# Slot bounds for four last sequences, chunk lists one by one, and another order of the first expert's start

## The reference

```python
x = layernorm(x + attention(x, w_q, w_k, w_v, w_o))   # 16 heads of 16 features
gates = softmax(x_flat @ gating_w)                    # 8 experts
topk_w, topk_idx = top_k(gates, 2)
position = cumsum(onehot(flat_e)) - 1                 # place of an entry in its expert's list
valid = position < capacity                           # capacity 1280
h = relu(einsum('ecd,edh->ech', buf, w1) + b1)        # hidden 1024
out_e = einsum('ech,ehd->ecd', h, w2) + b2
out_flat[flat_t] += out_e[flat_e, position] * w_eff   # 0 where not valid
x = layernorm(x + out_flat)
```

## Time and profile before

| | us |
|---|---|
| median of 3 runs (lowest, highest) | 818.85 (818.65, 819.21) |
| the profiled execution's own time | 818.66 |
| its span, first to last instruction | 816.8 |
| PE busy | 770.8 (94% of the span) |
| VectorE (DVE) busy | 605.0 (74%) |
| ScalarE (ACT) busy | 443.3 (54%) |
| GpSimd (POOL) busy | 406.4 (50%) |

### The profile page before, as it was taken

One profiled execution on the slowest core, in us unless ns is written; L12 is line 12 of the kernel. 1 busy time (PEld: TensorE's weight loads), 2 busy tenths in 40 slices (PEclk: granted clock), 3 DMA queues, 4 the chain that ended last, 5 costly groups with the idle time before them and its releaser, 6 DMA issues.

```text
span 816.8 us, 16628 instructions
## 1 busy us (share of the span) xinstructions
PE 770.8 (94%) x5919; PEld 642.9 (79%) x5919; DVE 605.0 (74%) x1325; ACT 443.3 (54%) x753; POOL 406.4 (50%) x595
## 2 busy tenths in 40 slices
PE   7689999999999988889999999999999999999993
PEld 6567777777777755778898898888988988988993
DVE  6757888888888898968657568568568567575982
ACT  3166777777777777645345345335435344444670
POOL 2000166665665547664364464462552553546774
PEclk9789999999999999999999999999999999999998
DMA  6567766565555672443352442452542532434841
GB/s 162 117 165 168 172 160 142 130 150 119 121 121 114 125 194 58 156 149 79 83 109 41 97 110 42 95 110 40 108 100 38 143 53 78 104 52 66 317 167 48
DMA packets 71535, 93.89 MB, mean 115 GB/s; under 512 B 11949, under 2 KB 55886, under 8 KB 71325
## 3 DMA queue, kind: packets, MB, share of 16 engines
q1 hardware_dynamic: 53308, 69.10, 32.1%
q0 software_dynamic: 16928, 22.15, 15.5%
q10 hardware_dynamic: 1216, 1.57, 0.8%
HBM read 39.76 MB, written 27.46 MB: 82 GB/s over the span
## 4 chain that ended last, share of the span: by engine, by line
PE 76%; DVE 12%; issue 4%; POOL 3%; DMA 2%; ACTq 1%; ACT 1%; POOLq 0%; DVEq 0%; SPq 0%
PE bank L1723 15%; PE bank L990 12%; DVE negm L895 10%; PE wide L1692 8%; PE wide L1690 8%; PE wide L1691 8%; PE bank L1725 8%; PE wide L1035 7%; PE bank L1669 2%; PE wide L1053 2%; PE bank L999 2%; PE bank L1100 1%; POOL slot_list L537 1%; POOL out L1420 1%; DMA rows<-x_rows,lists 1%
## 5 line engine op out<-in xcount | busy, mean ns | idle before, releaser
L1364 POOL DMA_INDIRECT acc_rows<-o_w,lists x70 | 117.1, 1672 | 177.3 <-ACT o_w L1513 163.6
L895 DVE TENSOR_REDUCE negm<-wide 128x4 f32<-128x1024 f32 x128 | 155.9, 1221 | 36.4 <-PE wide L1035 36.2
L634 ACT ACTIVATE probs<-wide 128x1024 f32<-128x1024 f32 x128 | 131.1, 1025 | 61.8 <-PE wide L1053 60.3
L1480 ACT ACTIVATE h<-wide,b1T 128x512 f32<-128x512 f32 (+1 forms) x200 | 115.4, 601 | 89.0 <-PE wide L1692 64.6
L1725 PE MATMUL bank<-stack,h_lo 128*128 128x256 f32 x560 | 156.4, 279 | 0.0
L1690 PE MATMUL wide<-g_hi,stack 128*128 128x512 f32 (+1 forms) x400 | 139.2, 348 | 0.8 <-ACT h L1480 0.7
L1692 PE MATMUL wide<-g_hi,stack 128*128 128x512 f32 (+1 forms) x400 | 138.9, 347 | 0.0
L1691 PE MATMUL wide<-g_lo,stack 128*128 128x512 f32 (+1 forms) x400 | 138.8, 347 | 0.0
L1513 ACT ACTIVATE o_w<-o_b,lists 128x256 f32<-128x256 f32 x70 | 35.7, 510 | 147.2 <-DVE o_b L1651 147.2
L1723 PE MATMUL bank<-stack,h_hi 128*128 128x512 f32 x304 | 108.0, 399 | 1.4 <-DVE o_b L1651 1.4
L1725 PEld LDWEIGHTS bank<-stack,h_lo 128*128 128x128 f32 x560 | 105.6, 189 | 0.0
(11 more groups left out here) (211 smaller groups left out, 1635.8 us busy)
## 6 DMA issues: line engine op xcount, KB each, us to landing
stack<-qk SPq DMA_DIRECT2D x180, 128.0 KB, 3.9
w_raw<-in_L_ffn_w SPq DMA_DIRECT2D x16, 1024.0 KB, 6.0
x_sb<-in_L_attn_x SPq DMA_DIRECT2D x16, 256.0 KB, 5.1
x_rows<-x SPq DMA_DIRECT2D x16, 256.0 KB, 3.7
acc_rows<-x SPq DMA_DIRECT2D x16, 256.0 KB, 3.9
acc_sb<-acc_rows SPq DMA_DIRECT2D x8, 512.0 KB, 8.9
out<-acc_sb SPq DMA_DIRECT2D x8, 512.0 KB, 2.6
x_rows<-zrow SPq DMA_DIRECT2D x2, 1152.0 KB, 6.2
```

Source lines behind the costliest of these rows:

```text
L634: nc.scalar.activation(probs[:, i % 4].rearrange("p x c t -> p x (c t)"), shifted_banks(i)[:, :, :], ACT.Exp, scale=SCALE).then_inc(exp_do ...
L895: nc.vector.tensor_reduce(negm[n % 2][:, :, :, u].rearrange("p c x -> p x c"), score_banks(PAIRS * n + u)[:, :, :].rearrange("p x (c t) -> ...
L1364: nc.gpsimd.indirect_dma_start(out=acc_d, out_offset=bass.IndirectOffsetOnAxis(ap=lists[:, e, QC * c + r, 0:1], axis=0), in_=o_w[c][:, r, ...
L1480: ins = nc.scalar.activation(h[u % 2][:, t], banks[BZ[u % 4]][:, t], ACT.Relu, bias=b1T[:, FT * e + f:FT * e + f + 1])
```

## The change

Four things change.

1. `STEPS` = 4: the slots of sequences 12, 13, 14 and 15 begin at 256, 512, 768 and 1024 or later. `slots` makes `gap` and `short` for sequences 14 and 15 too (two VectorE instructions for each), and TensorE the matmul of the count.
2. The lists of expert 0's five chunks are loaded one by one, chunk c once sequences 0 to 11 + c are listed: 0 and 1 where they were, 2 at turn END + LN[0] + 1 = 161, 3 and 4 after the turns. The three late chunks' common load goes.
3. GpSimd gathers chunk 2 at turn END - 8 + WRITE[1][2] = 162, behind the last two entry writes of sequence 14 and ahead of the four of sequence 15; chunks 3 and 4 after the turns, each behind its own list.
4. In `expert_order`, for expert 0, chunk 2 is taken in ahead of the whole of `layer2(0, 1)`, half of the second group's `layer1` too, and chunks 3 and 4 are taken in behind the other half of it.

```diff
@@ build
+    STEPS = NC - 1
-    chunk_v = [... for c in range(EC)]
+    chunk_v = [... for c in range(NC)]
@@ attention, sync_program
+            def load_chunk_list(c):
+                sequences = NB - STEPS + c
+                for i in range(2):
+                    sp.wait_ge(x1_stored[i], 32 * ((sequences + 1 - i) // 2))
+                for i in range(4):
+                    sp.wait_ge(listed[i], 16 * QC * TOPK * ((sequences + 3 - i) // 4))
+                sp.dma_start(lists[:, 0, QC * c:QC * c + QC]..., g["chunk_v"][c]).then_inc(chunk_listed[c], 16)
...
-                    for c, sequences in enumerate((FIRST - 1, FIRST)):
...
+                    for c in range(EC):
+                        load_chunk_list(c)
...
+                if turn == END + LN[0] + 1:
+                    load_chunk_list(EC)
...
-            for i in range(2):
-                sp.wait_ge(x1_stored[i], 32 * (NB // 2))
-            for i in range(4):
-                sp.wait_ge(listed[i], 16 * QC * TOPK * (NB // 4))
+            for c in range(EC + 1, NC):
+                load_chunk_list(c)
             late = g["late_v"]
-            sp.dma_start(lists[:, 0, EARLY // P:]..., late[:, 0]).then_inc(g["late0_loaded"], 16)
-            sp.dma_start(lists[:, 1:, EARLY // P:]..., late[:, 1:]).then_inc(g["late_loaded"], 16)
+            sp.dma_start(lists[:, 1:, EARLY // P:]..., late[:, 1:]).then_inc(g["lists_loaded"], 16)
@@ attention, gpsimd_program
+                if turn == END - 8 + WRITE[1][2]:
+                    gather(0, EC)
                 if turn == END + PV0 + 4:
                     pool.wait_ge(v_ready, QC * NB)
-                    pool.wait_ge(g["list0_loaded"], 16)
-                    gather(0, 0)
-                    pool.wait_ge(g["list1_loaded"], 16)
-                    gather(0, 1)
+                    for c in range(EC):
+                        gather(0, c)
@@ attention, slots
-                if m == FIRST - 1:
...
-                if m == FIRST:
...
+                step = m - (NB - STEPS)
+                if step >= 0:
+                    count = banks[pos_bank(m)][:, QC * NE:(QC + 1) * NE]
+                    nc.vector.tensor_scalar(gap[:, :], count, -1.0, float(CHUNK * (step + 1)), ALU.mult, ALU.add)...
+                    if step == 0:
+                        nc.vector.tensor_scalar(short[0][:, :], gap[:, :], 0.0, None, ALU.max)...
+                    else:
+                        nc.vector.tensor_tensor(short[step % 2][:, :], gap[:, :], short[1 - step % 2][:, :], ALU.max)...
@@ attention, tensor_program
-                    if m in (FIRST - 1, FIRST):
+                    if m >= NB - STEPS:
                         nc.tensor.matmul(banks[pos_bank(m)][:, QC * NE:(QC + 1) * NE], ones[:, :], seen[m % 2][:, :], ...)
@@ experts, gather
+                if e == 0:
+                    pool.wait_ge(g["chunk_listed"][c], 16)
@@ experts, gpsimd_program
-            pool.wait_ge(g["late0_loaded"], 16)
-            for n in range(EC, AHEAD):
-                gather(n // NC, n % NC)
-            pool.wait_ge(lists_loaded, 16)
-            pool.wait_ge(late_loaded, 16)
+            for c in range(EC + 1, AHEAD):
+                gather(0, c)
+            pool.wait_ge(lists_loaded, 16 * 2)
@@ expert_order
         if e == 0:
             layer2(0, 0)
-            layer2(0, 1, (0,))
             take_in(0, 2)
-            layer2(0, 1, (1,))
             layer1(0, second, (0, 1))
+            layer2(0, 1)
+            layer1(0, second, (2, 3))
             take_in(0, 3)
             take_in(0, 4)
-            layer1(0, second, (2, 3))
```

More of the change, by code:

```diff
@@ L74, in build @@
     early_v = by_expert[:, 0:EARLY, :].rearrange("e (p j) w -> p e (j w)", p=P)
-    chunk_v = [by_expert[0:1, c * C:(c + 1) * C, :].rearrange("e (p j) w -> p (e j w)", p=P) for c in range(EC)]
+    chunk_v = [by_expert[0:1, c * C:(c + 1) * C, :].rearrange("e (p j) w -> p (e j w)", p=P) for c in range(NC)]
     late_v = by_expert[:, EARLY:CAP, :].rearrange("e (p j) w -> p e (j w)", p=P)
@@ L97, in build @@
         w1_hi_done, w1_lo_done, w2_hi_done, w2_lo_done = sem("w1_hi_done"), sem("w1_lo_done"), sem("w2_hi_done"), sem("w2_lo_done")
-        list0_loaded, list1_loaded, lists_loaded, late0_loaded, late_loaded = (
-            sem("list0_loaded"), sem("list1_loaded"), sem("lists_loaded"), sem("late0_loaded"), sem("late_loaded"))
+        chunk_listed = [sem(f"chunk_listed{c}") for c in range(NC)]
+        lists_loaded = sem("lists_loaded")
         gathered = [sem(f"gathered{c}") for c in range(NC)]
@@ L172, in attention @@
     QC, DK, HH, NE, FT, FF, CAP, BLK = g["QC"], g["DK"], g["HH"], g["NE"], g["FT"], g["FF"], g["CAP"], g["BLK"]
-    SCALE, TRASH, TOPK = g["SCALE"], g["TRASH"], g["TOPK"]
+    SCALE, TRASH, TOPK, EC, NC = g["SCALE"], g["TRASH"], g["TOPK"], g["EC"], g["NC"]
     entry_d, HOPS = g["entry_d"], g["HOPS"]
@@ L313, in attention @@
         EARLY, FIRST = g["EARLY"], NB - LATE
+        CHUNK, STEPS = g["C"], g["STEPS"]
+        chunk_listed = g["chunk_listed"]
         END = 8 * (NB - 1)
@@ L377, in load_x @@
                 sp.dma_start(x_sb[n % XB][:, :, :], x_v[n]).then_inc(x_loaded[n % XB], 16)
+            def load_chunk_list(c):
[4 more added lines that the diff above has]
+                    sp.wait_ge(listed[i], 16 * QC * TOPK * ((sequences + 3 - i) // 4))
+                sp.dma_start(lists[:, 0, QC * c:QC * c + QC].rearrange("p j w -> p (j w)"), g["chunk_v"][c]).then_inc(chunk_listed[c], 16)
             for w, name in enumerate(("wq_d", "wk_d", "wv_d", "wo_d")):
@@ L438, in sync_program @@
                     sp.wait_ge(filled, 80)
-                    for c, sequences in enumerate((FIRST - 1, FIRST)):
-                        for i in range(2):
-                            sp.wait_ge(x1_stored[i], 32 * ((sequences + 1 - i) // 2))
-                        for i in range(4):
-                            sp.wait_ge(listed[i], 16 * QC * TOPK * ((sequences + 3 - i) // 4))
-                        sp.dma_start(lists[:, 0, QC * c:QC * c + QC].rearrange("p j w -> p (j w)"), g["chunk_v"][c]).then_inc(
-                            (g["list0_loaded"], g["list1_loaded"])[c], 16)
+                    for c in range(EC):
+                        load_chunk_list(c)
                     early = g["early_v"]
                     sp.dma_start(lists[:, 1:, 0:EARLY // P].rearrange("p e j w -> p e (j w)"), early[:, 1:]).then_inc(g["lists_loaded"], 16)
+                if turn == END + LN[0] + 1:
+                    load_chunk_list(EC)
                 if turn == END + PV0 + 7:
@@ L451, in sync_program @@
                                  g["b2_d"].rearrange("e d -> (e d)").partition_broadcast(P)).then_inc(g["b2_loaded"], 16)
-            for i in range(2):
-                sp.wait_ge(x1_stored[i], 32 * (NB // 2))
-            for i in range(4):
-                sp.wait_ge(listed[i], 16 * QC * TOPK * (NB // 4))
+            for c in range(EC + 1, NC):
+                load_chunk_list(c)
             late = g["late_v"]
-            sp.dma_start(lists[:, 0, EARLY // P:].rearrange("p j w -> p (j w)"), late[:, 0]).then_inc(g["late0_loaded"], 16)
-            sp.dma_start(lists[:, 1:, EARLY // P:].rearrange("p e j w -> p e (j w)"), late[:, 1:]).then_inc(g["late_loaded"], 16)
+            sp.dma_start(lists[:, 1:, EARLY // P:].rearrange("p e j w -> p e (j w)"), late[:, 1:]).then_inc(g["lists_loaded"], 16)
         def gpsimd_program(pool, gather):
@@ L822, in slots @@
                 dve.wait_ge(slot_done, m)
-                if m == FIRST - 1:
[L824 to L827, removed]
-                if m == FIRST:
[L829 to L833, removed]
+                step = m - (NB - STEPS)
+                if step >= 0:
+                    count = banks[pos_bank(m)][:, QC * NE:(QC + 1) * NE]
+                    nc.vector.tensor_scalar(gap[:, :], count, -1.0, float(CHUNK * (step + 1)), ALU.mult, ALU.add).then_inc(short_steps, 1)
+                    dve.wait_ge(short_steps, 3 * step + 1)
+                    if step == 0:
+                        nc.vector.tensor_scalar(short[0][:, :], gap[:, :], 0.0, None, ALU.max).then_inc(short_steps, 1)
+                    else:
+                        nc.vector.tensor_tensor(short[step % 2][:, :], gap[:, :], short[1 - step % 2][:, :], ALU.max).then_inc(short_steps, 1)
                 nc.vector.tensor_scalar(over[:, :, :], pos, float(CAP), float(NE * CAP), ALU.is_ge, ALU.mult).then_inc(over_done, 1)
@@ L838, in slots @@
                 beyond = over
-                if m >= FIRST - 1:
-                    steps = 2 if m < FIRST else 5 + m - FIRST
-                    dve.wait_ge(short_steps, steps)
+                if step >= 0:
+                    dve.wait_ge(short_steps, 3 * step + 2)
                     nc.vector.tensor_tensor(over_l[:, :, :], over[:, :, :],
-                                            short[int(m >= FIRST)][:, :].unsqueeze(1).to_broadcast([P, QC, NE]),
```

(4 more changed lines are left out.)

## The result

The changed kernel takes 826.05 us (median of 6 runs, 824.30 to 827.32), the kernel before 819.03 us (6 runs, 817.96 to 821.67). The ratio is 1.0087, 95% interval 1.0071 to 1.0103: slower by 7.1 us, twice the 3.6 us forecast and just above the range (820.3 to 825.5). The profiled execution took 824.89 us, with a span of 823.2.

What follows compares the result with a forecast made beforehand. PE was taken as the bound, through the third group's first matmul: new gaps of 3.5 and 2.8 us less old ones of 1.37 and 1.36 gave +3.6 on 818.85, so 822.4 us, range 820.3 to 825.5.

Steps and rivals of the forecast that it cites:

- the third group's first matmul: PE's `layer1` start for chunks 3 and 4, at 371.06 us before: any shift moves the end equally; forecast 374.7.
- the wait for rows: PE's gap before chunk 4's transposes, awaiting gathered rows: earlier lists and gathers were to remove it, -1.36 us.
- two gaps ended by g_lo: PE idle behind chunk 2's transposes, 3.5 us, and behind those of chunks 3 and 4, 2.8 us, until g_lo is done.
- From the end of the half of `layer1` to the third group: Second take-in: transposes of chunks 3 and 4, then a 2.8 us gap; from 371.12 to about 374.7.
- rival A: The worked-out case: new PE gaps without a clock fall, +3.6 us, 822.4 us, own range 821.0 to 823.3; chance 0.56.
- B: PE's clock falls in the new gaps, 2.0 us per fall: 824.4 with one, 826.4 with two; chance 0.24.
- VectorE's lateness, 0.56 us: Two added slot instructions each for sequences 14 and 15 delay VectorE up to `layer2(0, 0)`'s bias: +0.56 us, lower bound 0.

Runs made afterwards that it cites:

- changed again: The changed kernel, unaltered, measured once more on the same chip as later runs: 826.74 us in four runs, ratio 1.0108 to the kernel before.
- order alone: The kernel before with only the first expert's order changed; its own slots, lists and gathers kept: 826.08 us, ratio 1.0091.
- second take-in as before: The changed kernel with chunks 3 and 4 taken in ahead of the second half of chunk 2's `layer1`, as before the change: 821.38 us, ratio 1.0042.
- first gap filled: The changed kernel with 26 unread matmuls behind chunk 2's transposes, none behind those of chunks 3 and 4: 824.36 us, ratio 1.0073.
- run 1: The changed kernel with the first expert's old order put back; slots, lists and gathers stay changed: 819.42 us, ratio 1.0016 to the kernel before.
- run 4: The changed kernel with one tile of `layer2(0, 1)` between chunk 2's take-in and its `layer1`, the other tile after half of it: 818.09 us, ratio 0.9991.
- run 7: The changed kernel with GpSimd waiting for VectorE's bias of `layer2(0, 0)` before gathering chunk 3: 827.92 us, ratio 1.012, a single run.
- run 9: Changed lists and gathers, all of `layer2(0, 1)` behind chunk 2's take-in, first tile's bias earlier, `gap` and `short` as one instruction: 815.04 us, ratio 0.9954 to before.
- both gaps filled: The changed kernel with unread matmuls in both PE gaps, 26 behind chunk 2's transposes and 16 behind those of chunks 3 and 4: 822.66 us, ratio 1.0051.
- early bias: The kernel before with only VectorE's first-tile bias of `layer2(0, 0)` moved ahead of the last unit's conversions: 818.56 us, ratio 0.9997.

## Why the prediction was wrong

**What held.** That the third group's first matmul decides; that the wait for rows goes; that the order brings two gaps ended by g_lo, because ScalarE has `weigh` and VectorE the bias ahead; that the slots cost VectorE 0.56 us (from the transposes of chunk 1 to the last slot instruction: 342.88 - 335.94 = 6.94 us before, 343.36 - 335.81 = 7.55 after, so 0.61). From the end of the half of `layer1` to the third group it forecast 3.58 us, and 377.53 - 373.95 is 3.58.

**The step that failed: the clock.** The prediction took rival A, without a fall, at 0.56, and B, with one, at 0.24. The runs show B. In all five profiles with the long first gap unfilled (changed, changed again, order alone, second take-in as before, chunk 3 gathered later) the clock fell in the gap or little over a microsecond behind it. After the second gap (2.55 us) it fell in three of five (not in the changed kernel's two profiles; in those of the order alone, the first gap filled, and chunk 3 gathered later). The price in the changed kernel's profile: 5.30 instead of 2.86 us for the half of `layer1`, 2.4 us, where B had worked out 2.0; in the other four with a fall at the first gap the half took 4.29 to 5.20. Filling the gaps took 2.9 to 4.7 us off (1.0087 and 1.0108 against 1.0051). I weighed the one row in which PE stood for 5 us at the end and kept its clock more than the early one, in which it fell with 2.65 us of waiting. The Trainium skill's rule on gaps between bursts ("TensorE: Matmul & The Clock Gate", section "Why this matters for your kernels"), which the prediction had set beside B, would have made B's one fall, 824.4, the forecast. These traces agree with it at the first gap (3.75 to 4.54 us, five of five); that the clock also fell behind gaps of 2.55 us and, in run 1, of 1.92 us goes beyond it. One fall alone would not have met the time either: 824.4 is 1.6 us under the 826.05 measured.

**The term that was mis-sized: VectorE's lateness, 0.56 us.** It was 1.28: 0.61 for the slots, and 0.67 that the prediction did not have. From the last slot instruction to the bias VectorE takes 355.58 - 342.88 = 12.70 us before and 356.73 - 343.36 = 13.37 after:

```profile
342.88 0.17 DVE L847 TENSOR_TENSOR slot<-bank,over_l 128x16 f32<-128x16 f32 x1
...
355.58 0.42 DVE L1649 TENSOR_TENSOR low<-bank,b_all 128x256 f32<-128x256 f32 x1
```

```profile
343.36 0.17 DVE L849 TENSOR_TENSOR slot<-bank,over_l 128x16 f32<-128x16 f32 x1
```

The order is not the cause: with the order alone it is 12.68 us, and in all seven profiles with the changed lists and gathers, the old order and run 4's order among them, 13.35 to 13.37 (run 7 apart; run 9 moves the bias). The groups of the stretch from 344 to 357 us, before and after, show where (busy, mean ns):

```profile
L1558 DVE TENSOR_TENSOR h_lo<-h,h_hi 128x512 fp32r<-128x512 f32 x8 | 5.6, 706 | 0.3
L1556 DVE CAST h_hi<-h 128x512 fp32r<-128x512 f32 x8 | 3.7, 464 | 0.1
```

```profile
L1559 DVE TENSOR_TENSOR h_lo<-h,h_hi 128x512 fp32r<-128x512 f32 x8 | 5.9, 739 | 0.3
L1557 DVE CAST h_hi<-h 128x512 fp32r<-128x512 f32 x8 | 4.1, 514 | 0.1
```

Eight conversions of each kind: 8 x (0.050 + 0.033) = 0.66 us. GpSimd issues DMAs beside them for longer than before; run 7 took two of the issues away and got 0.28 back. The other 0.39 us are argued from the same slower conversions, not tested. So the chunk gathers that the change puts ahead do cost something, not on their own queue, but on VectorE.

**The sum again.** By distance: 3.64 forecast, + 0.73 for VectorE, + 2.44 for the fall, - 0.21 because the matmuls from 365.49 to 373.95 took 8.46 us instead of 8.67: 6.60, as measured. The time is another half microsecond up (7.1). Falls behind the second gap, at 1.6 to 1.8 us each in some of the runs, would make that up, but only the profiled runs could show them, and neither of the changed kernel's two has one. Without any fall the changed kernel is slower by 4.2 us (both gaps filled), which is A's 3.6 with the missing term.

**Left open.** Why the clock keeps its level over one gap of 2.55 us and not over another was not settled. Nor was it tried which of GpSimd's issues slows which conversion.

## What to carry to other kernels

When a take-in (transpose, convert, subtract) is put right ahead of the product that needs it, the wait is the whole way over the other engines plus what stands in their program order; put other matmuls between, one tile as in run 4 or two as in run 9. Reckon a gap of TensorE as its length plus the chance of a half-clock stretch behind it: here a fall at gaps of 3.75 to 4.54 us in five profiles of five, at 2.55 us in three of five, and at a price of 1.4 to 2.4 us each, up to two thirds of what both gaps themselves cost. If two limits stand one right behind the other, an edit against one alone may show no gain (0.9997 for the early bias, 1.0016 for the earlier lists in the old order); try them together (0.9954, with the other order and shorter `slots`).

## What the runs showed of the hardware

Idle TensorE time that can't be avoided can be filled to keep the clock: 42 unused matmuls made the kernel 2.9 us faster or more (ratios of 1.0087 and 1.0108 against 1.0051), and the granted clock stayed at 1.00 in the profile.

VectorE's conversions from SBUF to SBUF slow down beside GpSimd's indirect DMA issues: h_hi of 128x512 from 0.42 us to mostly 0.58 to 0.61, h_lo with its two inputs in SBUF from 0.69 to 0.74. Run 7 tested this for the last unit; for the others it is what stands side by side in the timelines. The Trainium skill ("SBUF — State Buffer", section "Who interferes with whom") says that a VectorE instruction in a two-port mode and one of GpSimd compete for a shared pair of ports, which the first to issue holds while the other blocks, and that a VectorE instruction with two SBUF inputs contends with GpSimd's reads. The direction agrees, though no view here shows the mode in which the casts ran. The size does not agree if an issue is taken to hold the ports for all of its 0.97 us, since no conversion waited that long.
